# A six-layer windowed-attention kernel: in stream 0 of TensorE's order, the second run of probabilities times values moves behind query/key chunks 2 and 3

## The reference

```
q, k, v = split(shift_tokens(x) @ Wqkv, 3)          # 16 heads of 64
q, k = l2norm(q) * q_scale, l2norm(k) * k_scale     # then rotary tables
sim  = q . k over windows of 32 queries x 64 keys, * 8, masked
out  = softmax(sim) @ v                              # "P times V"
x    = out @ Wo + x
x    = (a * gelu(gate)) @ W2 + b2 + x                # a, gate from layernorm(shift(x)) @ W1 + b1
```

## Time and profile before

| | |
|---|---|
| median of 3 runs | 1588.56 us |
| profiled execution: own time, span | 1589.05 us, 1587.3 us |
| TensorE matmul busy | 1504.4 us (95% of the span) |
| ScalarE busy | 1349.4 us (85%) |
| GpSimd busy | 1291.7 us (81%) |
| VectorE busy | 1277.5 us (80%) |
| granted TensorE clock, mean | 0.989 |

### The profile page before, as it was taken

How to read it: one execution, slowest core, us unless ns; L and a number is a source line. 1 busy time by engine, 2 the same in 40 slices (tenths; PEclk the granted TensorE clock), 3 DMA queues, 4 the chain that set the end, 5 groups by cost and what they waited for, 6 DMA issues and landing times.

```text
span 1587.3 us, 64246 instructions
## 1 busy us (share of the span) xinstructions
PE 1504.4 (95%) x26159; PEld 1311.9 (83%) x26159; DVE 1277.5 (80%) x2033; ACT 1349.4 (85%) x2600; POOL 1291.7 (81%) x1268
## 2 busy tenths in 40 slices
PE   5899998999999999999999999999999999999965
PEld 3688887888888888888888888888888888888855
DVE  6888887887888788788878878888888888888845
ACT  5779888988988888898889888989998898999853
POOL 8899899788879888898887889888799777777710
PEclk8999999999999999999999999999999999999988
DMA  4345343444333354333344343344433333333231
GB/s 138 85 114 126 81 99 74 112 109 113 95 84 78 91 127 113 91 92 93 82 114 126 90 95 85 91 120 113 105 90 87 95 85 77 78 84 78 65 83 29
DMA packets 217811, 150.44 MB, mean 95 GB/s; under 512 B 144556, under 2 KB 164656, under 8 KB 217520
## 3 DMA queue, kind: packets, MB, share of 16 engines
q1 hardware_dynamic: 217520, 146.33, 38.0%
HBM read 27.50 MB, written 1.05 MB: 18 GB/s over the span
## 4 chain that ended last, share of the span: by engine, by line
PE 85%; issue 5%; POOL 4%; ACT 4%; DVE 2%; DMA 0%; SPq 0%; POOLq 0%; ACTq 0%; DVEq 0%
PE ps_pv L872 12%; PE ps_tr L811 10%; PE ps_pv L904 10%; PE ps_s L851 8%; PE ps_qn L786 8%; PE ps_qn L788 7%; PE ps_qn L787 7%; PE ps_tr L798 5%; PE ps_pv L884 4%; PE ps_s L833 2%; PE ps_pv L922 2%; PE ps_pv L924 2%; PE ps_pv L923 2%; POOL qk L1999 2%; ACT pbd L1145 1%
## 5 line engine op out<-in xcount | busy, mean ns | idle before, releaser
L1999 POOL TENSOR_TENSOR qk<-qk,t 128x1024 f32<-128x1024 f32 x192 | 459.6, 2394 | 6.8 <-DVE qk L1524 6.6
L2011 POOL TENSOR_TENSOR qkr<-qk,rinv 128x1024 f32<-128x1024 f32 x192 | 363.9, 1907 | 3.7 <-POOL rinv L1983 0.2
L1521 DVE TENSOR_TENSOR t<-ps_qn,tab 128x512 f32<-128x512 f32 x384 | 261.1, 680 | 101.5 <-ACT sq L1157 98.1
L786 PE MATMUL ps_qn<-w_hi,xs_hi 128*128 128x512 f32 x576 | 251.9, 437 | 11.7 <-DVE qk L1524 9.3
L1524 DVE TENSOR_TENSOR qk<-ps_qn,tab 128x512 f32<-128x512 f32 x384 | 261.3, 681 | 0.0
L1145 ACT ACTIVATE pbd<-ps_tr 64x512 f32<-64x512 f32 x384 | 225.7, 588 | 31.8 <-PE ps_tr L798 28.5
L1157 ACT ACTIVATE sq<-ps_qn 128x512 f32<-128x512 f32 x384 | 229.7, 599 | 25.9 <-PE ps_qn L788 17.1
L787 PE MATMUL ps_qn<-w_lo,xs_hi 128*128 128x512 f32 x576 | 228.6, 397 | 0.8 <-issue 0.8
L788 PE MATMUL ps_qn<-w_hi,xs_lo 128*128 128x512 f32 x576 | 228.9, 397 | 0.0
L811 PE MATMUL ps_tr<-ident,qkr 128*128 128x128 f32 x1536 | 213.2, 275 | 11.5 <-ACT pbd L1145 8.5
L1534 DVE TENSOR_REDUCE ss<-sq 128x32 f32<-128x2048 f32 x96 | 218.5, 2276 | 0.0
(11 more groups left out here) (176 smaller groups left out, 3019.8 us busy)
## 6 DMA issues: line engine op xcount, KB each, us to landing
v_win<-v_new SPq DMA_DIRECT2D x576, 128.0 KB
v_win<-v_new SPq DMA_DIRECT2D x192, 64.0 KB
v_win<-v_win SPq DMA_DIRECT2D x188, 64.0 KB, 2.0
kT<-kT SPq DMA_DIRECT2D x84, 128.0 KB, 3.0
w_raw<-in_Wqkv SPq DMA_DIRECT2D x18, 512.0 KB, 3.9
rot<-in_rot SPq DMA_DIRECT2D x48, 128.0 KB
wo<-in_Wo SPq DMA_DIRECT2D x6, 512.0 KB, 4.8
x<-x SPq DMA_DIRECT2D x48, 56.0 KB
```

Of the source, the lines that this page charges most:

```text
L786: mm(ps_qn[bank][:, :], xs_hi[b][:, :], w_hi[:, part], start=True, stop=False)
L1521: v.tensor_tensor(t2[:, part].rearrange("p (h s d) -> p h s d", s=2, d=DH // 2), swapped, tab[:, 2 * k + 1:2 * k + 2, :].rearrange("p o (s ...
L1999: g.tensor_tensor(qk[b][:, part], qk[b][:, part], t2[:, part], ALU.add).then_inc(added[b], 1)
L2011: g.tensor_tensor(qkr[b][:, part].rearrange("p (h d) -> p h d", d=DH), qk[b][:, part].rearrange("p (h d) -> p h d", d=DH), rinv[b][:, k * ...
```

## The change

In stream 0, TensorE no longer runs both runs of probabilities times values in front of chunks 2 and 3. Run 0 stays there, and run 1 comes after chunk 3, directly in front of `transpose_mixed`. Stream 1 is as before, and so are the lists of all other engines and the orders of the rings' fills.

```diff
                     transpose_keys(i, b)
                     if b == 0:
                         probs_v(i, b, 0)
-                        probs_v(i, b, 1)
                     qkv(i, b, (2, 3))
                     if b == 1:
                         probs_v(i, b, 0)
-                        probs_v(i, b, 1)
+                    probs_v(i, b, 1)
```

## The result

The changed kernel takes 1640.28 us (median of 4 runs, 1638.75 to 1643.31) against 1587.14 us before (4 runs, 1582.60 to 1589.36). The ratio of the mean times is 1.0341, with a 95% interval of 1.0311 to 1.0371. The profiled execution took 1638.75 us, its span is 1637.0 us, at a mean granted clock of 0.99. That is 49.7 us over the profiled execution of before. The forecast was 1634 us, in a range of 1614 to 1652 us.

A forecast was written before the change was run, and what follows sets the result against it. TensorE's own list was taken as the bound, idle only 0.88 us a step. 37 x 0.9 + 2 x 1.25 + 7 x 1.35 = 45.3 us on 1589.05 us gave 1634 us, range 1614 to 1652 us.

The forecast's parts named there:

- gate late on VectorE: VectorE's gate after the first FFN chunk's gelu: starts 0.93 us late, at 806.66 instead of 805.73.
- per step, with the recurrence: Seven steps, 41 to 47, with the recurrence's rates: VectorE's lateness passes on in full, 1.35 us each.
- The stall: TensorE at L811, second four transposes of queries 1: waits 0.70 us for the bank ScalarE's mixed copies free.
- The switching: TensorE, behind chunk 3 and the mixed transpose: changing between kinds of matmuls costs 0.15 us per stream-0 half.
- The sum: Whole kernel: 37 x 0.9 + 2 x 1.25 + 7 x 1.35 = 45.3 us added, giving 1634 us.
- TensorE's busy time: Whole profile: TensorE's busy time should grow by little, with some 30 us of waits at L811.
- Weight loads ahead of running matmuls: Run 1 behind chunk 3: skill's rule would save 4.6 us of switching; prediction followed the trace's 0.33 us instead.
- What was covered: SyncE's value-window copy, 1.6 us later, and GpSimd's second sum, 1.25 us late: both hidden; clock stays at 1.00.
- Only the switching costs: Rival: ScalarE frees the mixed bank in time, TensorE pays only 7 us, 1596 us; 6 in 100.
- Everything compounds: Rival: VectorE's 1.25 us delays every step and stalls add up, above 1.35 us per step, 1652 to 1665 us; 7 in 100.
- The stall takes the place of idle time: Rival: TensorE's existing 0.88 us idle per step absorbs the stall, 1589 us within 3 us; 4 in 100.
- Faster: Rival: earlier chunks 2 and 3 shorten VectorE's wait for the square, 1549 or 1569 us; 3 in 100.

The follow-up runs named there:

- run 0: Not a follow-up kernel: the first of stream 0's two TensorE runs of probabilities times values, left in front of chunks 2 and 3; no time of its own.
- a1: Against the changed kernel, ScalarE's stream-0 order becomes run 0, squares 2 and 3, mixed copies, then run 1's evacuation; 1600.97 us, ratio 1.0089 to the kernel before.
- d1: Kernel before, TensorE's order unchanged, with six extra ScalarE copies ahead of run 1's evacuation in stream 0; 1630.71 us, ratio 1.0263.
- c1: Changed kernel with stream 0's run 1 placed between chunks 2 and 3 on TensorE, ScalarE's list the old one; 1599.23 us, ratio 1.0071 to the kernel before.
- h1: The change made in the 23 even steps only; 1615.59 us, ratio 1.0170 to the kernel before.
- a2: Changed kernel with ScalarE's stream-0 mixed copies moved ahead of run 1's evacuation, both squares behind it; 1656.99 us, ratio 1.0428 to the kernel before.
- b1: Kernel before, with ScalarE's mixed copies moved ahead of run 1's evacuation in stream 1 alone; 1583.11 us, ratio 0.9970.
- a3: Changed kernel with only square 2 moved ahead of run 1's evacuation on ScalarE in stream 0; 1614.32 us, ratio 1.0159 to the kernel before.

## Why the prediction was right

The mechanism, its place and its releaser were those forecast, and the time lay 6 us above the forecast. Step by step, in us from the start of run 0 where a time is given:

```
                                          forecast   measured
run 1 starts                                  2.60       2.69
square 2 starts                               4.27       4.44
second mixed copy ends                        5.20       5.38
stall ahead of the second four of L811        0.70       0.74
switching in the half                         0.15       0.31
FFN late                                      0.85       1.05
gate late on VectorE                          0.93       1.10
ScalarE's wait for run 1                      1.9        2.09
per step, middle layers                       0.9        1.09
per step, with the recurrence                 1.35       1.21
```

The last row is a difference of medians over steps 41 to 46; their mean is 1.05 us.

*The stall* was right to 0.04 us (2.13 against 1.39 in a1, whose order of TensorE is the same and which has no stall there). a1 and d1 show its cause from both sides.

*The switching* is the term that was mis-sized. I took one run as half of the 2.02 us of both and counted only the steps behind chunk 3 and behind the mixed transpose, 0.10 and 0.06 us. A run of 32 alone takes 1.08 to 1.09 us from start to start (826.18 to 827.27, 828.87 to 829.95), so splitting costs 1.09 + 1.08 - 2.02 = 0.15 us by itself. Over 46 halves the missed 0.16 us are 7 us. a1 and c1, which have switching without the stall, took 13 and 10 us more than the kernel before, with some of their delay lost in pauses.

*The sum* missed by less than its largest term did, and that is luck. From the starts of the mixed transposes, the profiled execution lost 38.5 us in the 37 steps from 4 to 40 (forecast 33.3), 3.6 us ahead of them (2.5) and 7.6 us from step 41 to the end (9.5): 49.7 us against 45.3. So the steps with the recurrence were priced too high, and that took back part of what the switching was priced too low.

*TensorE's busy time* was to grow by little. It grew by 25 us, and the wait that the profile puts down to the mixed copies is 21.9 us, not some 30: part of the loss stands in longer matmul records and on the weight-load side.

*Weight loads ahead of running matmuls.* The weight-load side idled 0.36 us in front of run 1 (it starts at 828.87, 0.33 us behind the last chunk matmul at 828.54), as the row of before had shown. The Trainium skill ("TensorE: Matmul & The Clock Gate", section "Architectural detail: the array is 16× 32×32, not 1× 128×128") has weight loads pulled ahead of matmuls in flight; at this place, behind a matmul that other instructions wait on and in front of one with waits of its own, no run here shows it.

*What was covered* stayed covered: the clock is 0.99 as before, the value chunks wait for VectorE no more than before, and GpSimd's wait for the rotation, 43.3 us now against 6.6 us, costs nothing, since GpSimd idles behind it for VectorE's statistics as before (ahead of `floored` 2.57 us in this half, 2.81 us in the half of the earlier trace rows).

*The rivals.* "Only the switching costs" is what a1 and c1 are; it needed another order on ScalarE or an earlier run 1. "Everything compounds" was named for VectorE's lateness; h1 shows no compounding, and a2 shows that VectorE's lateness does become a stall, at 1.9 us instead of 1.4 us. That was nearer than the forecast made it sound. "The stall takes the place of idle time" has fallen as the account of this change: a step is 1.09 us longer, with a stall of 0.74 us in it. A small part of it was there: pauses at the scores went from 14.3 to 11.2 us, and in c1 they took up more. "Faster" has fallen at its own sign: square 2 starts 4.44 us behind run 0, not ahead of the 3.02 us of before.

## What to carry to other kernels

Before moving a producer within one engine's list, look up where its consumer stands in the other engine's list: it is not the consumer that pays, but everything queued behind it. Lay out the one half step again with durations from the trace, find the first instruction behind the late one that somebody is due to wait for, and compare when it ends with when that engine arrives; here that gave the stall to 0.04 us. If the order of a producer is changed, change the consumer's order with it (a1 won back 39 of 53 us), and look for the same link where it is already late in the kernel as it stands (b1).

## What the hardware showed beyond that

A run of 32 matmuls of 64 columns takes 1.08 us from its start to the next instruction, and 64 of them 2.02 us: if a run costs a fixed part and the rest goes by its length, the fixed part is by estimate the 0.15 us from above, beside 0.10 us for its first instruction behind a 512-column matmul (0.33 us instead of 0.23 us). ScalarE's instructions that read PSUM were not equally long everywhere: the second mixed copy of stream 0 took 0.27 us before, 0.30 us in the changed kernel and 0.37 us in d1. TensorE has no matmul record at that time in the latter two. What goes with it is how much ScalarE did without a pause ahead of the mixed copies: no instruction since the last wait in the kernel before, a1 and a2 (0.27 us), one in a3 (0.28 us), two in the changed kernel and c1 (0.30 us), eight in d1 (0.37 us). Whether that is the cause was not tried.
